# A step order for each engine, high halves first, and hand-overs by blocks of 128 tokens in a four-layer graph network kernel

## The chip, the cores and the metric

The kernel runs on one core of one Trainium2 chip. The metric is the device time of one execution in microseconds, as the median of several runs.

## The reference

`x` has 128 batches of 64 nodes with 256 features. `adj` is one 64 x 64 matrix for all batches. Four layers follow one another, each inside a residual sum and a layer norm:

```python
x = _layernorm(x + _L0_gnn_ref(x, adj, ...))   # aggregate, dense 256->512, batch norm, relu, dense 512->256, batch norm
x = _layernorm(x + _L1_gnn_ref(x, adj, ...))   # L_norm @ x @ Wc, layer norm, relu; 4-head attention; layer norm; gelu MLP; layer norm
x = _layernorm(x + _L2_gnn_ref(x, adj, ...))   # two adj @ (x @ Wg) layers, then LSTMs over windows of 1, 2, 3 and 4 nodes
x = _layernorm(x + _L3_gnn_ref(x, adj, ...))   # graph attention: softmax of masked leaky-relu logits, times Wh
return x
```

The LSTMs run one after another over windows of p = 1 to 4 nodes; the last state of each window replaces the window's last node, so window length p reads what p - 1 wrote.

## The kernel before

**Stages.** Tokens (batch x node) are handled in tiles of 512. Two first stages do layer 0, whose batch norms need sums over all tokens; neither is touched by the change. The third stage, from 242 us to the end, does everything else for 16 tiles: two streams (`s` = 0, 1) of 8 tiles each (`n` = 1 to 8), each tile in two halves (`h` = 0, 1, written `.0` and `.1`) of 256 tokens, each half being two blocks `b` of 128 tokens.

**Products.** Operands of TensorE are pairs of fp16 numbers, a high half and a low half. `product` issues three matmuls for each product: high x high, high x low, low x high. ScalarE writes the high half of an activation from PSUM (`high`, L1447), VectorE then subtracts it and writes the low half (`low`, L1682), and TensorE waits for the low half before its first matmul. The LSTM states are split in the same way by VectorE alone (L1788, L1790 and L1796, the last two after the first).

**Steps and their order.** The work of a half tile is cut into steps: `turn_y` (transposes), `cheb` (the product with `L_norm`), `conv`, `turn_x1`, `v`, `q`, `k`, `scores`, `exps`, `turn_probs`, `attend`, `attn_out`, `turn_x2`, `mlp_up`, `mlp_down`, `mix0`, `gcn0`, `mix1`, `gcn1`, then for 11 LSTM cells c `inpC` (products with the input), `cellC` (products with the state, then gates) and `hidC` (new state), with `packC` for some, then `turn_state`, `turn_xc`, `gat`, `gat_keys`, `gat_exps`, `turn_att`, `gat_mix`, and the layer norms `norm_...`. An entry `1:conv.1` is step `conv` of stream 1, half 1; `+` in place of `:` means the stream's next tile. One list, written out by hand, gives the order for all engines: every engine walks through `OPENING`, seven times through `ROUND` and through `CLOSING`, and does its own part of each step. The engines wait for one another by semaphores (`Signal`); each engine's own instructions run in the order of the list. The two streams are about half a tile apart, so that one has attention while the other has LSTM cells.

**Hand-overs.** A signal covers a half tile where the change touches it: `ln_apply` on VectorE (L1642, two instructions, one for each block) signals after the second, and the TensorE step that reads both blocks waits for it. The same holds for `make_x2` (L1661), for the masked logits (L1811), the exponentials (L1538, ScalarE) and `take_att` (L1544, one copy for both blocks) of graph attention. `gat_mix` (L1393) writes both blocks of a half to one PSUM bank.

Of the kernel before, what the change touches and what calls it, by code (L numbers as in the profile page):

```python
# [82 lines left out]
1:attn_out.0 0:pack4.0 0:hid7.1 1:norm_g2.0 1:mlp_up.1 0:inp8.1 1:gelu_split.1 0:inp7.0 0:cell8.1 1:turn_x2.0
1:mlp_down.1 0:cell7.0 0:hid8.1 0:inp9.1 0:hid7.0 1:norm_g3.1 1:mlp_up.0 1:gelu_split.0 0:cell9.1 1:norm_l1.1 0:inp8.0
0:hid9.1 0:cell8.0 1:mlp_down.0 1:mix0.1 0:inp10.1 0:hid8.0 1:norm_g3.0 0:cell10.1 1:gcn0.1 0:hid10.1 1:norm_l1.0
0:inp9.0 0:cell9.0 1:mix1.1 0:hid9.0 0:turn_state.1 0:inp10.0 1:gcn1.1 0:cell10.0 0:norm_l2.1 0:hid10.0 1:mix0.0
1:inp0.1 0:turn_xc.1 0:turn_state.0 1:cell0.1 1:gcn0.0 0:gat.1 0:norm_l2.0 1:mix1.0 0:gat_keys.1 1:hid0.1 0:turn_xc.0
0:gat_exps.1 1:gcn1.0 1:inp1.1 0:turn_att.1 1:cell1.1 0:gat_mix.1 1:hid1.1 0:gat.0 0:norm_l3.1 1:inp0.0 0+turn_y.1
1:cell0.0 0:gat_keys.0 1:inp2.1 1:cell2.1 0+norm_l0.1 0:gat_exps.0 1:hid0.0 1:hid2.1 1:inp1.0 0:turn_att.0 0+cheb.1
1:cell1.0 0:gat_mix.0 1:inp3.1 1:hid1.0 0:norm_l3.0 0+conv.1 0+turn_y.0 1:cell3.1 1:inp2.0 0+norm_l0.0 0+norm_g1.1  # L90
1:cell2.0 0+cheb.0 1:hid2.0 0+xa_bias.1 1:inp3.0 0+conv.0 0+turn_x1.1 0+norm_g1.0 1:cell3.0 0+v.1 0+xa_bias.0 0+q.1
# [11 lines left out]
0+hid2.1 0+inp3.1 1:norm_l3.1 1+norm_g1.0 0+inp2.0 0+cell2.0 1+turn_y.1 0+cell3.1 1+norm_l0.1 0+hid2.0 0+hid3.1  # L103
0+inp3.0 1+xa_bias.0 1+turn_x1.0
""".split()
ROUND = [(int(entry[0]), int(entry[1] == "+"), entry[2:]) for entry in ROUND]


OPENING = """
# [1824 lines left out]
```

## Time and profile before

| | |
|---|---|
| median of 3 runs | 2045.37 us (2044.44 to 2046.44) |
| the profiled execution, its time | 2043.5 us |
| its span | 2041.7 us |
| TensorE busy in the span | 1947.0 us, 95% |
| VectorE busy | 1721.9 us, 84% |
| ScalarE busy | 1449.9 us, 71% |
| mean granted TensorE clock | 0.994 |

PE is TensorE's matmuls and PEld its weight loads, which run beside them. DVE is VectorE, ACT ScalarE, POOL GpSimd. A matmul's bar is drawn from its start to its modelled end, and bars of successive matmuls overlap.

### The profile page before, as it was taken

What the parts mean: (1) busy time and instruction counts of PE and PEld (TensorE: products, weight loads), DVE (VectorE), ACT (ScalarE), POOL (GpSimd) and SP (SyncE); (2) the same over time, 40 slices, a digit from 0 to 9 for tenths busy, and PEclk for the clock granted to TensorE, in tenths of its full rate; (3) what the DMA queues carried; (4) which work ended last, traced back from release to release, by engine and by line L of the source; (5) the groups of instructions that cost most, each with busy time, mean ns of one, the idle gap of its engine ahead of it and who ended that gap; (6) DMA issues with size and microseconds to landing.
All of it is one profiled execution on the core that took longest, in us unless ns stands there. A gap on an engine that the chain in (4) does not pass through costs nothing.

```text
span 2041.7 us, 85679 instructions
## 1 busy us (share of the span) xinstructions
PE 1947.0 (95%) x37031; PEld 1729.0 (85%) x37031; DVE 1721.9 (84%) x4795; ACT 1449.9 (71%) x4443; POOL 185.9 (9%) x258
## 2 busy tenths in 40 slices
PE   6999879999999999999999999999999999999997
PEld 3444458989998999999998999899989999899996
DVE  6779787889888988898888988898889888888866
ACT  5657536777777787768777777677776777677677
POOL 2000010010101000100011010101010001011000
PEclk9999989999999999999999999999999999999999
DMA  7857400000100001000100010000100010000000
GB/s 283 289 184 267 155 2 23 13 13 3 44 3 23 3 3 44 13 13 3 44 14 13 3 44 3 23 3 3 44 13 13 3 44 13 13 4 13 3 3 23
DMA packets 36822, 87.79 MB, mean 43 GB/s; under 512 B 2416, under 2 KB 26992, under 8 KB 32752
## 3 DMA queue, kind: packets, MB, share of 16 engines
q1 hardware_dynamic: 36464, 82.56, 11.6%
q8 instruction: 280, 4.59, 0.9%
q14 instruction: 78, 0.64, 0.1%
HBM read 52.15 MB, written 30.41 MB: 40 GB/s over the span
## 4 chain that ended last, share of the span: by engine, by line
PE 69%; DVE 11%; ACT 5%; issue 2%; POOL 1%; DVEq 0%; ACTq 0%
PE ps L282 21%; PE ps L284 20%; PE ps L283 20%; ACT pool_mem L1498 2%; DVE stats L1632 2%; PE ps L296 2%; PE ps L1157 2%; PE ps L1240 1%; ACT xb L1434 1%; PE ps L1265 1%; DVE pool_mem L1785 1%; POOL rstd L1596 1%; DVE mv L1636 1%; PE ps L1393 1%; DVE t L1826 1%
## 5 line engine op out<-in xcount | busy, mean ns | idle before, releaser
L1498 ACT ACTIVATE pool_mem<-ps,lstm_b 128x64 f32<-128x64 f32 (+2 forms) x2496 | 610.9, 356 | 96.3 <-PE ps L284 91.9
L282 PE MATMUL ps<-hl_a,w_hi 128*128 128x64 f16 (+2 forms) x3776 | 540.4, 214 | 18.0 <-DVE hl_a L660 16.1
L283 PE MATMUL ps<-hl_a,w_hi 128*128 128x64 f16 (+2 forms) x3776 | 539.5, 214 | 0.0
L284 PE MATMUL ps<-hl_a,w_lo 128*128 128x64 f16 (+2 forms) x3776 | 539.5, 214 | 0.0
L282 PEld LDWEIGHTS ps<-hl_a,w_hi 128*128 128x128 f16 x3776 | 349.2, 97 | 46.1 <-DVE hl_a L660 17.2
L284 PEld LDWEIGHTS ps<-hl_a,w_lo 128*128 128x128 f16 x3776 | 348.8, 97 | 23.0 <-issue 0.7
L283 PEld LDWEIGHTS ps<-hl_a,w_hi 128*128 128x128 f16 x3776 | 348.9, 97 | 22.5 <-issue 0.6
L282 PE MATMUL ps<-hl_b,w_hi 128*128 128x84 f16 (+2 forms) x2112 | 366.0, 228 | 0.3
L283 PE MATMUL ps<-hl_b,w_hi 128*128 128x84 f16 (+2 forms) x2112 | 366.3, 228 | 0.0
L284 PE MATMUL ps<-hl_b,w_lo 128*128 128x84 f16 (+2 forms) x2112 | 365.0, 228 | 0.0
L282 PE MATMUL ps<-pool_mem,w_hi 128*128 128x64 f16 (+2 forms) x3072 | 352.9, 200 | 0.1
L283 PE MATMUL ps<-pool_mem,w_hi 128*128 128x64 f16 (+2 forms) x3072 | 352.6, 200 | 0.0
L284 PE MATMUL ps<-pool_mem,w_lo 128*128 128x64 f16 (+2 forms) x3072 | 352.2, 200 | 0.0
L1596 POOL TENSOR_TENSOR rstd<-mv,nhalf 128x2 f32<-128x2 f32 x224 | 172.1, 770 | 1624.1 <-DVE mv L1636 1624.1
L282 PEld LDWEIGHTS ps<-pool_mem,w_hi 128*128 128x128 f16 x3072 | 284.9, 98 | 2.7 <-DVE pool_mem L1790 0.2
L283 PEld LDWEIGHTS ps<-pool_mem,w_hi 128*128 128x128 f16 x3072 | 286.8, 98 | 0.5
L284 PEld LDWEIGHTS ps<-pool_mem,w_lo 128*128 128x128 f16 x3072 | 285.0, 98 | 0.0
L282 PEld LDWEIGHTS ps<-hl_b,w_hi 128*128 128x128 f16 x2112 | 207.1, 98 | 18.3 <-DVE hl_b L1682 2.0
L284 PEld LDWEIGHTS ps<-hl_b,w_lo 128*128 128x128 f16 x2112 | 206.2, 98 | 14.9
L283 PEld LDWEIGHTS ps<-hl_b,w_hi 128*128 128x128 f16 x2112 | 205.6, 97 | 15.2
L1507 ACT ACTIVATE pool_mem<-pool_mem 128x256 f32<-128x256 f32 (+2 forms) x352 | 128.3, 374 | 82.3 <-DVE pool_mem L1766 44.5
L1632 DVE BATCH_NORM_STATS2 stats<-t 128x6 f32<-128x256 f32 x448 | 168.3, 418 | 5.5
(237 smaller groups left out, 4207.4 us busy)
## 6 DMA issues: line engine op xcount, KB each, us to landing
xa<-in_x SPq DMA_DIRECT2D x32, 512.0 KB, 5.5
h_scratch<-pool_mem SPq DMA_DIRECT2D x14, 1024.0 KB, 4.3
pool_mem<-h_scratch SPq DMA_DIRECT2D x14, 1024.0 KB, 7.0
pool_mem<-in_wpack SPq DMA_DIRECT2D x16, 704.0 KB, 4.2
out<-xb SPq DMA_DIRECT2D x16, 512.0 KB, 3.4
...
```

The source lines that it names most:

```text
L282: nc.tensor.matmul(o, l[0], r[0], start=first, stop=False, skip_group_check=True)
L283: nc.tensor.matmul(o, l[0], r[1], start=False, stop=False, skip_group_check=True)
L284: return nc.tensor.matmul(o, l[1], r[0], start=False, stop=last, skip_group_check=True)
L296: mm = nc.tensor.matmul(to(f, batch)[c, :], of(f)[n, c], matrix[n, n], start=True, stop=True)
L1157: mm = nc.tensor.transpose(fea(s, bank)[:, f, b * P:(b + 1) * P], src[s][:, h * HALF + b, f * P:(f + 1) * P], ident[:, :])
L1240: mm = nc.tensor.matmul(to[half, b, pair, batch * NODES:(batch + 1) * NODES], q[s][h][d, pair, at_b:at_b + NODES], kk[s][h][d, pair, at_b: ...
L1265: mm = nc.tensor.matmul(ps[s][d, banks[batch], c:c + NODES], vv[s][h][k, b, head * HEAD_DIM:(head + 1) * HEAD_DIM], prob_tr[s][h][k, b, pa ...
L1393: mm = nc.tensor.matmul(tok(s, BANK_A[h])[:, b, :], att_tr[s][h][:, b, :], wh[s][h][:, b, :], start=True, stop=True)
L1498: op = nc.scalar.activation(gates[s][h][:, g, m * w:(m + 1) * w], gate_place(s, h, g, m, w), ACT.Tanh, bias=lstm_b[:, bias:bias + 1], scal ...
L1507: nc.scalar.activation(cell_t[s][h][:, 0:KT * w], cell_c[s][h][:, 0:KT * w], ACT.Tanh, scale=0.5)\
L1596: nc.gpsimd.tensor_tensor(rstd[s][:, blocks(h)], mv[s][:, blocks(h), 1], nhalf[:, 0:HALF], ALU.pow)\
L1632: nc.vector.bn_stats(stats[s][:, b, 0:6], t[s][:, b, :]).then_inc(ln_step.of(s, h), 1)
```

## The change

The three lists become one dictionary `ORDER` with a list for each of PE, ACT, DVE and POOL. Each list has three parts: the first for tile 1, the second for each of tiles 2 to 6, and the third for tiles 7 and 8, which are now ordered together. The steps are the same, and so are the matmuls and their number. The middle part keeps every engine's old order apart from local shifts: of PE's 164 entries none moves by more than four places, of the 178 of ScalarE only `norm_y` by more than four (13 later for stream 0, 57 earlier for stream 1), of the 204 of VectorE only `1:cell3.1` by more than five (13 later).

```diff
-ROUND = """
-1:cheb.1 0:pack3.1 0:cell3.0 0+norm_y 1:conv.1 0:inp4.1 0:hid3.0 1:norm_g1.1 0:cell4.1 1:v.0 0:pack3.0 1:q.0 1:k.0
...
+ORDER = {
+    "PE": ("""
+0:turn_y.1 0:turn_y.0 1:turn_y.1 0:cheb.1 1:turn_y.0 0:conv.1 0:cheb.0 0:conv.0 0:turn_x1.1 0:v.1 0:q.1 0:k.1
+0:turn_x1.0 0:scores.1 1:cheb.0 0:v.0 0:q.0 0:k.0 1:cheb.1 0:scores.0 0:turn_probs.1 0:attend.1 0:attn_out.1
+0:turn_probs.0 1:conv.0 0:attend.0 0:turn_x2.1 0:attn_out.0 0:mlp_up.1 1:conv.1 0:turn_x2.0 0:mlp_down.1 0:mlp_up.0
...
+1:cheb.1 0:cell3.0 1:conv.1 1:v.0 1:q.0 1:k.0 0:inp4.1 1:scores.0 1:turn_x1.1 0:inp4.0 1:v.1 1:q.1 1:k.1 0:inp5.0
+1:scores.1 0:inp5.1 0:cell5.1 0:cell5.0 1:turn_probs.1 1:turn_probs.0 0:inp6.1 1:attend.0 1:attend.1 0:cell6.1
...
+1:inp0.0 0:gat_keys.0 0+turn_y.1 1:inp2.1 1:inp1.0 0:turn_att.0 0+cheb.1 0:gat_mix.0 1:inp3.1 0+conv.1 0+turn_y.0
+1:inp2.0 1:cell3.1 0+cheb.0 1:inp3.0 0+turn_x1.1 0+conv.0 1:cell3.0 0+v.1 0+q.1 0+turn_x1.0 0+k.1 0+v.0 0+scores.1
...
+1:turn_xc.0 1:cell10.1 1:gat.0 0+gcn0.0 1:gat_keys.0 1:turn_state.1 0+mix1.0 0+gcn1.1 0+gcn1.0 1:turn_att.0
+1:gat_mix.0 1:turn_xc.1 0+inp0.1 1+turn_y.0 0+inp0.0 1:gat.1 0+inp1.1 1:gat_keys.1 1+cheb.0 0+inp1.0 1+conv.0
...
+    begin, again, end = ORDER[engine]
+    steps = at(begin, 1)
+    for r in range(2, ROUNDS - 1):
+        steps += at(again, r)
+    return steps + at(end, ROUNDS - 1)
...
+                        wait_hi(k)
+                        for b in range(HALF):
                             a = first + b * P
-                            mm = product(tok(s, bank)[:, b, :], (src[:, 0, k, a:a + P], src[:, 1, k, a:a + P]),
-                                         weight(name, k, 0, DIM), k == 0, k == kts - 1 and with_row is None)
...
+                            for part in range(2):
+                                nc.tensor.matmul(tok(s, bank)[:, b, :], hi, w[part], start=k == 0 and b == 0 and part == 0,
+                                                 stop=False, skip_group_check=True)
...
+                    for k in range(kts):
+                        wait_lo(k)
+                        for b in range(HALF):
+                            a = first + b * P
+                            mm = nc.tensor.matmul(tok(s, bank)[:, b, :], src[:, 1, k, a:a + P], weight(name, k, 0, DIM)[0],
+                                                  start=False, stop=k == kts - 1 and b == HALF - 1, skip_group_check=True)
...
+                    def wait_hi(k):
+                        if k == 0:
+                            pe.wait_ge(*(feat_lo if which in MIX_BANK else feat_hi).at(s, n, h, which))
...
-                    pe.wait_ge(*cell_dve.at(s, n, h, f"{c - 1}.lo"))
+                    pe.wait_ge(*cell_dve.at(s, n, h, f"{c - 1}.hi"))
+                    low_ok = cell_dve.at(s, n, h, f"{c - 1}.lo")
...
-                    pe.wait_ge(*gat_ok.at(s, n, h, "exps"))
                     for b in range(HALF):
-                        mm = nc.tensor.transpose(gat_bank(s, h, b)[:, TILE - P:TILE], att[s][h][:, b, :], ident[:, :])
-                    mm.then_inc(gat_ps.of(s, h), 1)
+                        pe.wait_ge(*gat_ok.at(s, n, h, f"exps{b}"))
+                        nc.tensor.transpose(gat_bank(s, h, b)[:, TILE - P:TILE], att[s][h][:, b, :], ident[:, :])\
+                            .then_inc(gat_ps.of(s, h), 1)
...
-                        op = nc.vector.tensor_scalar(dst[s][:, b, :], t[s][:, b, :], mv[s][:, b, 0:1], rstd[s][:, b:b + 1],
-                                                     ALU.subtract, ALU.mult)
-                    op.then_inc(ln_out.of(s, h), 1)
+                        nc.vector.tensor_scalar(dst[s][:, b, :], t[s][:, b, :], mv[s][:, b, 0:1], rstd[s][:, b:b + 1],
+                                                ALU.subtract, ALU.mult).then_inc(ln_out.of(s, h), 1)
```

`rows_of`, `gat_dense`, `cell_input` and `cell_state` are split like `dense`: first all matmuls that read the high half, behind a wait for it, then those that read the low half, behind a wait of their own. For the four operands of `MIX_BANK` (`xp`, `o`, `m0`, `m1`) both waits stay on the low half, because the product writes a PSUM bank that VectorE still reads for it. `turn` and `mix` wait for each block of `l0`, `l1`, `l2` and `x2` separately; `gat_keys`, `turn_att`, `take_att`, the exponentials and `gat_mix` signal by block, and `gat_mix` writes block b to bank `gat_bank(s, h, b)`. `take_att` becomes two copies of 128x128.

## Rows read from the trace of the kernel before

**Rows 1.** The page: span, then each engine's busy time; last the chain that ended last.
```profile
span 2041.7 us, 85679 instructions
...
PE 1947.0 (95%) x37031; PEld 1729.0 (85%) x37031; DVE 1721.9 (84%) x4795; ACT 1449.9 (71%) x4443; POOL 185.9 (9%) x258
...
PE 69%; DVE 11%; ACT 5%; issue 2%; POOL 1%; DVEq 0%; ACTq 0%
```
**Rows 2.** Busy us of each engine by stretch: two rounds, third stage's start and end.
```profile
745.71:965.20 219.49, 215.26 (x4386) 202.38 (x4385) 191.18 (x553) 162.59 (x529) 21.62 (x28) 1.00 0.06 17
...
1184.64:1404.10 219.46, 215.24 (x4386) 202.38 (x4385) 191.14 (x553) 162.63 (x529) 21.62 (x28) 1.00 0.06 17
...
1843.00:2041.70 198.70, 182.29 (x3812) 172.03 (x3810) 152.70 (x468) 145.41 (x502) 15.84 (x21) 0.98 0.03 11
...
240.00:306.81 66.81, 46.58 (x546) 36.15 (x545) 51.80 (x135) 21.95 (x41) 7.92 (x11) 0.87 0.03 9
```
**Rows 3.** PE's waits in the round 745.71 to 965.2: total us, times, longest.
```profile
PE ps L1157 <- DVE x L1642: 0.9, 2, 0.7
PE ps L1240 <- ACT pool_mem L1462: 0.8, 1, 0.8
PE ps L1387 <- ACT pool_mem L1538: 0.7, 1, 0.7
PE ps L296 <- ACT t L1484: 0.6, 1, 0.6
PE ps L296 <- DVE xa L1642: 0.5, 2, 0.3
PE ps L1393 <- ACT pool_mem L1544: 0.5, 1, 0.5
```
**Rows 4.** Timeline around one of these waits: start, us, engine, line.
```profile
895.26 0.27 PE L283 MATMUL ps<-hl_b,w_hi 128*128 128x256 f16 x1
895.37 0.27 PE L284 MATMUL ps<-hl_b,w_lo 128*128 128x256 f16 x1
895.68 0.60 ACT L1462 ACTIVATE pool_mem<-ps 128x512 f32<-128x512 f32 x1 [0.36 <-PE ps L284]
...
896.42 0.69 PE L1240 MATMUL ps<-pool_mem 64*64 64x64 f32 x32 [0.78 <-ACT pool_mem L1462]
```
**Rows 5.** The round's groups by line and shape, busy us, mean ns.
```profile
L282 PEld LDWEIGHTS ps<-hl_a,w_hi 128*128 128x128 f16 x448 | 41.3, 97 | 0.5
...
L1682 DVE TENSOR_TENSOR hl_b<-ps,hl_b 128x512 f16<-128x512 f32 x16 | 11.0, 686 | 1.9 <-ACT hl_b L1447 1.9
...
L1538 ACT ACTIVATE pool_mem<-pool_mem,smin 128x128 f32<-128x128 f32 x9 | 3.6, 416 | 0.9 <-DVE smin L1811 0.8
...
L1642 DVE TENSOR_SCALAR x<-t,mv,rstd 128x256 f32<-128x256 f32 x8 | 2.9, 409 | 1.4 <-POOL rstd L1596 1.4
```
**Rows 6.** PE's waits from 240 to 306.8 us.
```profile
PE ps L282 <- DVE hl_a L1682: 5.5, 3, 2.4
PE ps L1157 <- DVE x L1700: 3.6, 1, 3.6
PE ps L296 <- DVE xa L1642: 3.1, 1, 3.1
PE ps L1157 <- DVE x L1661: 2.2, 2, 1.4
PE ps L282 <- DVE hl_b L1682: 1.8, 1, 1.8
PE ps L282 <- DVE pool_mem L1738: 1.2, 1, 1.2
```
**Rows 7.** PE's waits from 1850 us to the end, the longest.
```profile
PE ps L1148 <- DVE pool_mem L1785: 1.8, 2, 1.0
PE ps L1157 <- DVE x L1661: 1.6, 1, 1.6
PE ps L282 <- DVE hl_b L1682: 1.6, 1, 1.6
```
**Rows 8.** Timeline at the start of `turn_probs` of stream 1.
```profile
800.41 0.69 DVE L1722 TENSOR_TENSOR pool_mem<-pool_mem,ssum 128x512 f32<-128x512 f32 x1
...
801.11 0.86 PEld L1250 LDWEIGHTS ps<-ident,pool_mem 128*128 128x128 f32 x8
```
**Rows 9.** Timeline of the last layer norm and store.
```profile
2034.30 4.04 ACT L1434 ACTIVATE xb<-t,nmr,rstd 128x256 f32<-128x256 f32 x8 [1.73 <-DVE nmr L1668]
...
2036.40 2.35 SPq L1117 DMA_DIRECT2D out<-xb  x2
```

More of the change, by code:

```diff
@@ L1 @@
+import itertools
 from contextlib import ExitStack
@@ L83 @@
[L83 to L91, printed above, removed]
-0+turn_x1.0 1:hid3.0 0+k.1 1:hid3.1 0+scores.1 1:pack3.0 0+v.0 0+exps.1 0+q.0 1:pack3.1 0+k.0 1:inp4.0 1:cell4.0
@@ L103 @@
[L103 to L109, printed above, removed]
-0+norm_y 0+turn_y.1 0+norm_l0.1 0+turn_y.0 0+cheb.1 0+norm_l0.0 0+conv.1 1+norm_y 0+norm_g1.1 0+cheb.0 0+xa_bias.1
-0+turn_x1.1 0+conv.0 0+v.1 0+q.1 0+norm_g1.0 0+k.1 0+xa_bias.0 0+scores.1 0+turn_x1.0 1+turn_y.0 0+exps.1 0+v.0
-1+norm_l0.0 0+q.0 0+k.0 0+turn_probs.1 0+scores.0 0+attend.1 0+exps.0 0+attn_out.1 0+norm_g2.1 0+turn_probs.0
@@ new lines @@
+0:inp9.0 0:cell9.0 1:mix1.1 0:inp10.0 0:turn_state.1 0:cell10.0 1:gcn1.1 1:mix0.0 0:turn_xc.1 1:inp0.1 0:gat.1
+0:turn_state.0 0:gat_keys.1 1:gcn0.0 1:inp1.1 1:mix1.0 0:turn_att.1 0:turn_xc.0 0:gat_mix.1 1:gcn1.0 0:gat.0
+1:inp0.0 0+turn_y.1 0:gat_keys.0 1:inp2.1 1:inp1.0 0+cheb.1 0:turn_att.0 1:inp3.1 0:gat_mix.0 0+conv.1 1:inp2.0
+0+turn_y.0 1:cell3.1 0+turn_x1.1 1:inp3.0 0+cheb.0 0+v.1 0+conv.0 0+q.1 1:cell3.0 0+k.1 0+turn_x1.0 0+scores.1 0+v.0
+0+q.0 0+k.0 1:inp4.0 0+scores.0 0+turn_probs.1 1:inp5.0 0+attend.1 1:cell5.0 0+attn_out.1 0+turn_probs.0 1:inp4.1
@@ new lines @@
+1:cell8.1 1:hid8.1 1:turn_state.0 1:norm_l2.0 1:cell9.1 1:hid9.1 1:turn_xc.0 0+mix1.0 1:cell10.1 1:hid10.1
+1:gat_keys.0 0+mix1.1 1:turn_state.1 1:norm_l2.1 1:gat_exps.0 0+gcn1.1 1:gat_mix.0 1:turn_xc.1 1:norm_l3.0 0+cell0.1
+0+gcn1.0 1+turn_y.0 0+hid0.1 1+norm_l0.0 1:gat_keys.1 0+cell1.1 1+cheb.0 0+cell0.0 1:gat_exps.1 0+hid1.1 0+hid0.0
+1+conv.0 0+cell1.0 1:gat_mix.1 0+cell2.1 0+hid1.0 1:norm_l3.1 0+hid2.1 1+norm_g1.0 0+cell2.0 1+turn_y.1 0+hid2.0
+1+norm_l0.1 0+cell3.1 1+xa_bias.0 0+hid3.1 1+turn_x1.0
@@ new lines @@
+1:turn_state.0 1:cell9.1 1:norm_l2.0 1:hid9.1 1:turn_xc.0 0+mix0.0 1:cell10.1 1:hid10.1 0+mix1.1 1:gat_keys.0
+0+mix1.0 1:turn_state.1 1:gat_exps.0 1:norm_l2.1 0+gcn1.1 1:gat_mix.0 0+gcn1.0 1:norm_l3.0 1:turn_xc.1 0+cell0.1
+1+turn_y.0 0+cell0.0 0+hid0.1 1+norm_l0.0 0+hid0.0 0+cell1.1 1+cheb.0 1:gat_keys.1 0+hid1.1 1+conv.0 0+cell1.0
+1:gat_exps.1 0+cell2.1 1:gat_mix.1 0+hid1.0 0+hid2.1 1:norm_l3.1 1+norm_g1.0 0+cell2.0 1+xa_bias.0 1+turn_y.1
+0+cell3.1 1+norm_l0.1 0+hid2.0 0+hid3.1 1+turn_x1.0
@@ L1183, in dense @@
[L1183 to L1193 removed]
+                            hi, w = src[:, 0, k, a:a + P], weight(name, k, 0, DIM)
@@ L1413, in _ @@
                 keep_clock(ps[1][:, 2, :], 6)
[L1414 to L1419 removed]
+                for name, s, n in steps_of("PE"):
                     run(name, s, n)
```

533 lines of the change are left out of this document (358 added, 175 removed).

## The prediction

> **What bounds the kernel now.** I read the page first. Of the span of 2041.7 us TensorE's matmuls fill 95%, VectorE 84% and ScalarE 71%, and the chain that ended last lies on TensorE for 69% [rows 1]. TensorE is the bound, and a change that leaves its matmuls as they are can only take time out of its pauses. The change touches the third stage alone, so I then cut that stage by stretches [rows 2]. A round of the steady part takes 219.5 us, twice alike, with matmuls busy for 215.3: 4.2 us idle. The start, 240 to 306.8 us, has 46.6 us busy out of 66.8, at a mean granted clock of 0.87: 20.2 us idle, and about 0.13 x 66.8 = 8.7 us of clock withheld, which costs only where PE works. The end, from 1843 us, has 182.3 of 198.7: 16.4 us idle. Between 306.8 us and about 2000 us lie some 7.7 rounds.
>
> Third, the view of waits says which pause ends on what. In a steady round it has six groups, eight waits, 4.0 us together [rows 3]. None of them is a wait for a low half: ScalarE's or VectorE's last instruction of another kind ends each. At the start the low halves do appear: 5.5 us of `hl_a`, 1.8 of `hl_b` and 1.2 of `pool_mem` at L1738, out of 17.4 shown [rows 6]. At the end there is 1.6 [rows 7].
>
> The waits are too small by one piece each. In the timeline the last matmul before `scores` starts at 895.37 us. Its like follow one another after 0.11 us, yet its bar is 0.27 long, and `scores` starts at 896.42 [rows 4]. So 1.05 - 0.11 = 0.94 us were lost where the view counts 0.78: 0.16 us more for each wait. Eight waits then cost 4.0 + 8 x 0.16 = 5.3 us a round.
>
> **The change, part by part.** It removes no matmul and adds none; both parts of a product keep their weight loads.
>
> (a) The step order and the block hand-overs in a steady round. I go through [rows 3] with the new lists beside them.
> The 0.8 of `scores` behind `take_k` (L1462): the new PE list has `0+v.0` between `0+k.1` and `0+scores.1`, twelve matmuls of 0.11 us, 1.3 us of work. The wait goes.
> The 0.9 behind L1642 is `turn_xc` after `norm_l2`: `1:gat_mix.0` now comes before `1:turn_xc.1`, and the first block is signalled one instruction of 0.41 us earlier [rows 5]. About 0.3 is left.
> The 0.7 behind L1538 is `turn_att` after the exponentials: its first block is signalled one activation of 0.42 us earlier [rows 5], and the masked logits before it by one instruction. About 0.1 is left.
> The 0.6 behind L1484 is `mix1` after `gcn_relu`: `1:turn_state.1`, four transposes of 0.11 us each [rows 8], moves in front of `0+mix1.0`. About 0.15 is left.
> The 0.5 behind `xa` is `cheb` after `norm_l0`, two waits of 0.3 or less, and a block is 0.41 us earlier. About 0.1 is left.
> The 0.5 behind L1544 is `gat_mix` after `take_att` of half 1: `1:gcn1.0` now stands between. But `1:turn_att.0` and `1:gat_mix.0` now stand side by side where `turn_xc.1` had been between, and the copy, though halved, has to be waited for. About 0.45 stays.
> Kept 1.1 of 4.0; saved 2.9, and for four or so waits that vanish 4 x 0.16 = 0.6: 3.5 us a round. Over 7.7 rounds 27 us. The bounds are nothing (each wait comes back elsewhere) and all 5.3 us, 41 us.
>
> (b) High halves first. A low half of 512 elements takes VectorE 0.69 us [rows 5], and TensorE may now start that much sooner after the high half. In the steady round no wait ends on a low half [rows 3], because other steps of the hand-made order stand in between and hide the 0.69 us. So I book nothing there; what hides it is TensorE's own work, and if the tighter rounds of (a) use up that cover, the earlier start is what keeps the wait from appearing. Where TensorE does wait for one, at the start for `hl_b` and `pool_mem`, I book two times 0.7 = 1.4 us [rows 6]. The largest, 5.5 us for `hl_a`, is `xp` and `o`, which belong to `MIX_BANK` and still wait for their low half: nothing.
>
> (c) The start. The new PE list moves one `turn_y`, `cheb.0`, `cheb.1`, `conv.0` and `conv.1` of stream 1 into places where stream 0's chain had left TensorE idle. A `conv` is twelve matmuls of 0.11 us, 1.3 us, a transpose or mixing step some 0.7: together 4.7 us of work that no longer has to be done later. Signals by block take 0.4 us from each of three waits, for `xa` and L1661 [rows 6]: 1.2. With (b) that is 7.3 us. Against it, VectorE is already busy for 51.8 of 66.8 us there [rows 2], and the layer norm that goes before a moved `cheb` costs it some 3 us, in front of stream 0's own chain in the same queue. I take 2 us off: 5 us saved. ScalarE's `norm_y` of the next tile of stream 0 now stands early, behind `cheb.1`. It needs the first load, for which the queue waits only until both `turn_y` are done, and it is two ScalarE instructions in a stretch where that engine is busy 22 of 67 us [rows 2]: nothing. The bounds for the start are minus 3 us (VectorE's work wholly in the chain) and 20 us (all idle time).
>
> (d) The end. Tiles 7 and 8 in one list let stream 0's last cells fill stream 1's gaps. The last layer norms and the store, 2034.3 us to the end, 7.4 us, stay [rows 9], so of 16.4 us idle 9 can be had; waits of 1.8, 1.6 and 1.6 lead them [rows 7]. I take 3 us, with bounds of 0 and 9.
>
> (e) Added work. `take_att` becomes two copies, one more ScalarE instruction for each half tile, 32 in all. ScalarE is idle for 57 us of a round [rows 2]: nothing.
>
> The Trainium skill has a rule that speaks against the signals by block: "TensorE: Matmul & The Clock Gate", section "The cost: per-tile semaphore tail", gives 26.3 ns for each increment that a matmul makes and advises one on the last. The change has 12 more a round, by that figure an estimated 0.3 us a round and 2.5 us over the kernel; no run here shows it yet, and the sum leaves it out.
>
> **Sum.** 27 + 5 + 3 = 35 us. The profiled execution took 2043.5 us, so 2008.5. Its time lies 1.9 us below the median of the runs, so for the median 2010 us. The bounds of the terms add up to minus 3 and 41 + 20 + 9 = 70 us, 1975 to 2048.
>
> **Rivals.** One: half of the gain comes back. When TensorE's round shrinks to 216 us, VectorE is busy for 191 of it [rows 2], 89%, and both it and ScalarE have in-order queues. Each handover that they make late shows up as a new short wait. For it: four of the six groups of waits already end on ScalarE or on VectorE work behind it, not on any missing TensorE work. Against it: VectorE and ScalarE get lists of their own, so a ready instruction is less often held behind another. The price is half of the 27 us or more: 2024 to 2041 us.
>
> Two: there is more to gain than the waits show. Weight loads are busy 202.4 us of a round, so 17.1 us have none [rows 2], four times the idle time of the matmuls. Some of that is not a pause: a load takes 0.097 us [rows 5] under a matmul of 256 columns that takes 0.11. If half of the 13 us that the two figures differ by is real pause, and high-first and the new lists take half of that, 3 us a round more go, 25 us in all: about 1985 us, and below.
> The Trainium skill, "Perfetto Trace Analysis", section "Identifying the Most-Contended Engine", says that matmul busy share is a poor measure of how near TensorE is to its limit and that weight loads are the better one; it is the page for this rival. By matmuls a round could give 4.2 us, by loads up to 17.1.
>
> Three: it gets slower. The lists of different engines contradict each other in places. In the middle part PE does `1:turn_probs.1` before `1:turn_probs.0`, while VectorE and ScalarE make `exps.0` and `turn_probs.0` first. Before, the last multiplication ended at 801.10 us and the eight transposes began at 801.11 without a wait, half 0 first [rows 8]: what is now asked for first had 0.4 us to spare, four transposes. With nothing ready behind it, TensorE waits for all of the difference. A place of this kind costs 0.7 us, a VectorE instruction [rows 5]. It takes more than five of them a round before the 3.5 us saved are lost, and with eight a round is 2.1 us longer, 16 us in all: 2053 us once the 8 us of start and end are taken off. It decides from the sixth on.
>
> Four: no change, 2041.3 to 2049.5 us. A measurement tells 0.2%, 4.1 us, from nothing. All the terms would have to be at their low ends.
>
> **Chances.** My forecast, 1990 to 2024 us: 0.60. Rival one, 2024 to 2041: 0.17. Rival two, below 1990: 0.10. No change: 0.05. Slower: 0.08. Faster by over 0.2% is 0.60 + 0.17 + 0.10 = 0.87. Leaving out some 0.07 at the low side, the part of rival two below 1983, and some 0.13 above, the two last cases, the range is 1983 to 2040 us.
>
> **What the profile after would show.** A round of 215 to 217 us between repeats of one instruction; PE's waits in it without L1240 and L1484, those for L1642 and L1538 below 0.4, and one for the copy of `take_att` of stream 1 half 0. In the start, from 242 us to the first LSTM gates, a stretch 4 to 7 us shorter with less time at the half clock. The number of matmuls the same, 37031. The prediction is wrong if the round is not shorter (rivals one and three: look for new waits, `turn_probs` first), or shorter by more than 6 us (rival two: pauses that the matmul bars had hidden).

## The result, and the profile after

The changed kernel takes 2014.85 us, the median of 4 runs (2013.94 to 2015.3), against 2044.9 us of the kernel before (4 runs, 2044.25 to 2046.44): a ratio of 0.9852, with a 95% interval of 0.9838 to 0.9866. It is 30.0 us faster. The forecast was 2010 us, a gain of 35. The profiled execution took 2013.94 us, at a mean granted clock of 0.996 (0.994 before).

The page of the changed kernel: span, busy times, and the chain that ended last by engine.

```profile
span 2012.1 us, 85711 instructions
...
PE 1944.8 (97%) x37031; PEld 1730.6 (86%) x37031; DVE 1718.2 (85%) x4795; ACT 1443.6 (72%) x4475; POOL 187.8 (9%) x258
...
PE 78%; ACT 5%; DVE 4%; issue 1%; POOL 0%; ACTq 0%; DVEq 0%
```

Beside [rows 1] the matmuls are the same 37031, and the busy times of TensorE, VectorE and ScalarE stay within 0.5% (GpSimd's within 1%); ScalarE has the 32 instructions more that the halved copies make. VectorE's share of the last chain falls from 11% to 4%, TensorE's rises from 69% to 78%. Of the 29.6 us by which the span shrank, TensorE's idle time gives 27.4 and its busy time 2.2: its work stayed the same, its pauses shrank.

Windows of the changed kernel: a steady round from one instruction to its repeat, then the same 66.8 us at the start as in [rows 2], and last a stretch of about the same length at the end. The columns are those of [rows 2]. The next round, to 1276.60 us, takes 215.72 us.

```profile
845.17:1060.88 215.71, 214.54 (x4386) 202.70 (x4384) 190.91 (x553) 161.93 (x533) 21.84 (x28) 1.00 0.06 18
...
240.00:306.81 66.81, 51.82 (x681) 40.19 (x680) 58.60 (x153) 26.78 (x50) 10.37 (x13) 0.92 0.08 25
...
1813.00:2012.10 199.10, 182.44 (x3798) 172.31 (x3796) 150.41 (x466) 144.53 (x507) 15.35 (x21) 0.98 0.03 11
```

This round takes 215.7 us where it took 219.5, and TensorE's idle time in it falls from 4.2 to 1.2 us. The start now holds 681 matmuls in the 66.8 us that held 546, at a mean granted clock of 0.92 instead of 0.87. The last 199 us look as before: 16.7 us idle, 16.4 before.

TensorE's waits in this round, all of them:

```profile
PE ps L1330 <- DVE x L1859: 0.6, 1, 0.6
PE ps L1627 <- ACT pool_mem L1772: 0.2, 1, 0.2
```

These two lines answer to the six of [rows 3]. L1330 is `turn_xc` behind `norm_l2`. L1627 is `gat_mix` behind the copy of `take_att`, at 949 us, where `1:turn_att.0` and `1:gat_mix.0` stand side by side. The waits of `scores`, `mix1`, `cheb` and `turn_att` are gone. No wait stands at `turn_probs`, the place that rival three named.

The timeline around the longer one shows who is late.

```profile
1058.10 0.69 DVE L1898 TENSOR_TENSOR hl_b<-ps,hl_b 128x512 f16<-128x512 f32 x1
...
1058.70 0.72 DVE L1859 TENSOR_SCALAR x<-t,mv,rstd 128x256 f32<-128x256 f32 x2
...
1059.16 0.33 PE L1330 MATMUL ps<-ident,x 128*128 128x128 f32 x1 [0.65 <-DVE x L1859]
```

TensorE needs the first block of a layer norm (L1859), and VectorE makes the low half of another stream's product (L1898, 0.69 us) ahead of it. Block hand-over shows too: TensorE starts at 1059.16, before the second of the two instructions ends at 1059.42.

TensorE's waits from 240 to 306.8 us, the longest and those of the kinds that stood in [rows 6]:

```profile
PE ps L1353 <- DVE hl_a L1898: 5.3, 5, 1.8
PE ps L468 <- DVE xa L1859: 2.5, 1, 2.5
...
PE ps L1330 <- DVE x L1916: 0.8, 1, 0.8
...
PE ps L1353 <- ACT pool_mem L1707: 0.8, 2, 0.4
...
PE ps L1330 <- DVE x L1877: 0.4, 1, 0.4
PE ps L1363 <- DVE hl_b L1898: 0.4, 1, 0.4
```

The 5.3 us for `hl_a` are the low halves of `xp` and `o` and, at 298.66 us, of `m0`, which still are waited for. (The prediction put the 5.5 us of [rows 6] down to `xp` and `o` alone; the third of them, at 305.38 us, is `m0`, which belongs to `MIX_BANK` as well.) The 1.2 for the gelu's low half became 0.8 for its high half (ScalarE's L1707), and the 1.8 for `hl_b` 0.4. The 3.6 and 2.2 us behind VectorE's L1700 and L1661 became 0.8 and 0.4 (L1916 and L1877).

TensorE's waits from 1850 us to the end, the longest, and then the last layer norm and the store in the timeline:

```profile
PE ps L1320 <- DVE pool_mem L2002: 2.6, 2, 2.3
PE ps L1330 <- DVE x L1877: 2.0, 1, 2.0
PE ps L1627 <- ACT pool_mem L1772: 1.2, 2, 1.0
```
```profile
2003.15 4.04 ACT L1662 ACTIVATE xb<-t,nmr,rstd 128x256 f32<-128x256 f32 x8 [0.98 <-DVE nmr L1884]
...
2007.21 0.93 SPq L1289 DMA_DIRECT2D out<-xb  x2
```

The three longest are no shorter than those of [rows 7]; all of the view together are 6.0 us against 7.4. The last layer norm's eight instructions take 4.04 us on ScalarE as in [rows 9], but what follows does not stay. In [rows 9] the first store is issued 2.10 us after the first of the eight starts, here 4.06 us after it. ScalarE's old list ends `0+norm_l3.1 0+norm_l3.0 1+norm_l3.1 1+norm_l3.0`, so stream 0's tile is complete after four of the eight; the new one ends `0+norm_l3.1 1+norm_l3.1 1+norm_l3.0 0+norm_l3.0`, and a store needs both halves of its tile. From the first of the eight to the end are 9.0 us where there were 7.4.

**Where the 30 us lie.** From the two traces, from instruction to its repeat, and last from that layer norm to the end of the span:

| stretch | before | after | difference |
|---|---|---|---|
| third stage's start to the first `gcn` relu | 65.1 | 59.7 | -5.4 |
| from there to the first `norm_l3` | 120.1 | 117.1 | -3.0 |
| five repeating rounds | 5 x 219.48 | 5 x 215.96 | -17.6 |
| the round after them | 219.4 | 217.1 | -2.3 |
| from there to the last layer norm | 290.2 | 288.7 | -1.5 |
| from the last layer norm to the end | 7.4 | 9.0 | +1.6 |
| the third stage | 1799.7 | 1771.4 | -28.3 |

The third stage starts at 242.0 us before and at 240.7 after. Both executions run the same code up to there, and in other executions it starts at up to 244.7, so these 1.3 us, which with the 28.3 make the 29.6 of the spans, are no part of the change. The start's own length also varies: from the stage's first instruction to the first `gcn` relu, two kernels below with the same first lists take 62.1 and 64.2 us (e1 and e6), and four with the new ones 57.6 to 59.7 (e5, e8, e9 and the changed kernel).

### The profile page after: what moved, and what is told of

Its sections match the earlier page's. It is cut to its first block, busy times and chain, and to the rows that moved or that the text cites. A ratio compares the mean times of both kernels' runs of the same rounds, so it can differ in the third digit from the quotient of the medians.

```text
span 2012.1 us, 85711 instructions
## 1 busy us (share of the span) xinstructions
PE 1944.8 (97%) x37031; PEld 1730.6 (86%) x37031; DVE 1718.2 (85%) x4795; ACT 1443.6 (72%) x4475; POOL 187.8 (9%) x258
## 4 chain that ended last, share of the span: by engine, by line
PE 78%; ACT 5%; DVE 4%; issue 1%; POOL 0%; ACTq 0%; DVEq 0%
PE ps L1539 18%; PE ps L1568 11%; PE ps L1548 9%; PE ps L1353 8%; PE ps L1387 7%; PE ps L1575 5%; PE ps L1363 4%; PE ps L1395 3%; PE ps L468 2%; PE ps L1330 2%; ACT pool_mem L1726 2%; PE ps L1320 1%; PE ps L1627 1%; PE ps L1595 1%; PE ps L1441 1%; DVE stats L1849 1%
## 5 line engine op out<-in xcount | busy, mean ns | idle before, releaser
L1539 PE MATMUL ps<-hl_a,w_hi 128*128 128x64 f16 (+1 forms) x3584 | 361.3, 205 | 1.8 <-DVE hl_a L2005 0.9
L1539 PE MATMUL ps<-hl_a,w_lo 128*128 128x64 f16 (+1 forms) x3584 | 360.8, 205 | 0.0
L1539 PEld LDWEIGHTS ps<-hl_a,w_hi 128*128 128x128 f16 x3584 | 284.4, 97 | 6.3 <-DVE hl_a L2005 1.2
L1568 PE MATMUL ps<-pool_mem,w_hi 128*128 128x64 f16 (+2 forms) x3072 | 273.6, 200 | 0.0
L1548 PE MATMUL ps<-hl_a,w_hi 128*128 128x64 f16 (+1 forms) x3584 | 233.5, 205 | 0.2 <-issue 0.2
L1568 PEld LDWEIGHTS ps<-pool_mem,w_hi 128*128 128x128 f16 x3072 | 228.9, 98 | 2.9
L1548 PEld LDWEIGHTS ps<-hl_a,w_hi 128*128 128x128 f16 x3584 | 177.4, 97 | 0.9 <-issue 0.3
L1575 PE MATMUL ps<-pool_mem,w_hi 128*128 128x64 f16 (+2 forms) x3072 | 175.4, 200 | 0.0
L1983 DVE SCALAR_TENSOR_TENSOR pool_mem<-pool_mem 128x256 f32<-128x256 f32 (+2 forms) x352 | 118.8, 340 | 38.7 <-ACT pool_mem L1726 36.4
L1387 PE MATMUL ps<-hl_b,w_hi 128*128 128x256 f16 x640 | 150.3, 273 | 0.4 <-DVE hl_b L1898 0.2
L1387 PE MATMUL ps<-hl_b,w_lo 128*128 128x256 f16 x640 | 150.2, 273 | 0.0
L2002 DVE SCALAR_TENSOR_TENSOR pool_mem<-pool_mem 128x256 f32<-128x256 f32 (+2 forms) x352 | 123.9, 356 | 28.9 <-ACT pool_mem L1735 27.8
L1575 PEld LDWEIGHTS ps<-pool_mem,w_hi 128*128 128x128 f16 x3072 | 135.9, 98 | 0.0
L1539 PE MATMUL ps<-hl_b,w_hi 128*128 128x84 f16 x1408 | 130.4, 201 | 0.5
L1539 PE MATMUL ps<-hl_b,w_lo 128*128 128x84 f16 x1408 | 130.5, 200 | 0.0
```

The costliest lines, as they stand in the source:

```text
L1387: nc.tensor.matmul(out[:, j, :], w[part], hi[:, k, :], start=j == 0 and k == 0 and part == 0, stop=False, skip_group_check=True)
L1539: nc.tensor.matmul(o, wk[part], toks[0][:, k], start=(g, m) == gms[0] and k == 0 and part == 0, stop=False, skip_group_check=True)
L1548: mm = nc.tensor.matmul(o, weight(f"wih{p}", k, (g * KT + m) * P, P)[0], toks[1][:, k], start=False, stop=step == 0 and (g, m) == gms[-1] ...
L1568: nc.tensor.matmul(gate_place(s, h, g, m, w), wk[part], hi[:, k * w:(k + 1) * w], start=False, stop=False, skip_group_check=True)
L1575: mm = nc.tensor.matmul(gate_place(s, h, g, m, w), weight(f"whh{p}", k, (g * KT + m) * P, P)[0], lo[:, k * w:(k + 1) * w], start=False, st ...
L1983: nc.vector.scalar_tensor_tensor(cc if first else g[GATE_I], g[GATE_I], 1.0, g[GATE_G], ALU.add, ALU.mult).then_inc(cell_dve.of(s, h), 1)
```

## The experiments

Each experiment takes the changed kernel and edits it, and none leaves out any of the computation. "Round" is the mean of the five repeating rounds in the trace.

### The first four: which part of the change carries the gain

`e1_old_order` puts back the old lists and keeps high-first and the blocks:

```diff
-ORDER = {... "PE": ("""0:turn_y.1 0:turn_y.0 1:turn_y.1 0:cheb.1 1:turn_y.0 ...
+ORDER = {... "PE": ("""0:turn_y.1 0:turn_y.0 0:cheb.1 0:conv.1 0:cheb.0 ...   (all four lists cut from the old ROUND)
```

> The changed kernel with the one hand-written step order of before put back on all engines; high halves first and hand-overs by block stay. Theory (the step orders carry most of a round's gain, block hand-overs some, high halves first next to nothing in a round): only what the block signals shorten is kept, about 0.4 us for each of the waits behind L1642, L1538 and xa, 1.2 to 1.6 us a round, 9 to 12 us, and 2 to 3 us at the start: 2031 to 2035 us, a round of 218 us. Rival (high halves first carries it): most of the 30 us stay, 2015 to 2023 us. Rival (nothing without the new orders): 2042 to 2045 us.

`e2_low_first` keeps the lists and the blocks, and lets each high matmul wait for the low half, as before:

```diff
-    pe.wait_ge(*(feat_lo if which in MIX_BANK else feat_hi).at(s, n, h, which))
+    pe.wait_ge(*feat_lo.at(s, n, h, which))
...
-    pe.wait_ge(*cell_dve.at(s, n, h, f"{c - 1}.hi"))
+    pe.wait_ge(*cell_dve.at(s, n, h, f"{c - 1}.lo"))
...
-    pe.wait_ge(*gelu_hi.at(s, n, h, f"m{k + KT - 1}"))
+    pe.wait_ge(*gelu_lo.at(s, n, h, "m23" if k else "m01"))
```

> The changed kernel, but TensorE waits for the low half before the first matmul of each product, as before the change; the new order of the matmuls inside a product, the new step orders and the hand-overs by block stay. Theory: the low halves were hidden in a round, so a round stays within 0.3 us of 215.7 and only the start loses 1.4 us: 2016 to 2019 us. Rival (the new step orders are tighter and need the earlier start): each product of a short cycle waits up to 0.7 us, 1 us or more a round, 2023 us or more.

`e3_half_signals` keeps the lists and high-first; each wait for a block becomes a wait for the second block:

```diff
-    turn(s, n, h, xc, "xc", lambda b: pe.wait_ge(*ln_out.at(s, n, h, f"l2.{b}")))
+    turn(s, n, h, xc, "xc", lambda b: pe.wait_ge(*ln_out.at(s, n, h, "l2.1")))
...
-    pe.wait_ge(*gat_ok.at(s, n, h, f"exps{b}"))
+    pe.wait_ge(*gat_ok.at(s, n, h, "exps1"))
```

> The changed kernel, but every wait for a block waits for the second block of the half tile (layer norms l0, l1, l2, x2, keys, masked logits, exponentials, take_att, gat_mix); the instructions and their signals stay as they are. Theory: the waits that remain in a round grow by up to 0.4 us each, 0.8 to 1.2 us a round, and the start by 1 us: 2021 to 2025 us. Rival (blocks are worth nothing, since other work hides the 0.4 us): 2014 to 2016 us.

`e4_order_alone` is the new lists with the edits of both e2 and e3.

> The new step orders alone: both undoings of the two runs before together. Theory: 2022 to 2028 us, the two losses add up, and with the run on the old order the three parts sum to the whole 30 us within 5 us. Rival (the parts need one another): above 2035 us, or the sum of the parts misses the whole by 10 us or more.

Measured, all four on one chip, against 2045.97 us of the kernel before there:

| kernel | median us | ratio (95%) | round us |
|---|---|---|---|
| e1_old_order | 2037.22 | 0.9964 (0.995 to 0.9978) | 218.85 |
| e2_low_first | 2070.44 | 1.0119 (1.0103 to 1.0134) | 222.4 |
| e3_half_signals | 2028.58 | 0.9914 (0.9901 to 0.9928) | 217.11 |
| e4_order_alone | 2080.95 | 1.0171 (1.0157 to 1.0185) | 223.4 |

All four missed the ranges expected of them: e1 by 2 us and e3 by 4, e2 and e4 by over 50. e2 and e4 refuted the theory behind the prediction. Without high-first the new lists are not a little less good, they lose 25 us to the kernel before, and without the blocks 35 us. TensorE's waits in a round of e2 say why:

```profile
PE ps L1353 <- DVE pool_mem L1940: 1.8, 3, 0.8
PE ps L1531 <- DVE hl_a L1883: 1.7, 3, 0.8
PE ps L1330 <- DVE x L1844: 0.6, 1, 0.6
PE ps L1557 <- DVE pool_mem L1992: 0.6, 2, 0.4
PE ps L1531 <- DVE hl_a L1998: 0.4, 1, 0.4
PE ps L1353 <- DVE hl_b L1883: 0.3, 1, 0.3
PE ps L1612 <- ACT pool_mem L1757: 0.2, 1, 0.2
```

Five of these seven lines, ten waits and 4.8 us, or 6.4 us with 0.16 more for each, end on a low half made by VectorE: of the gelu (L1940), of `h1`, the input of the LSTM windows of one node (`hl_a`, L1883; TensorE's L1531 is in `cell_input`), of `x1` in front of `v` (`hl_b`, L1883), of the LSTM state (L1992, L1998). In [rows 3] there is none of this kind. The round is 6.4 us longer than the changed kernel's 215.96. The new lists put products closer behind what feeds them: between `1:gcn1.1`, from which `h1` comes, and `1:inp0.1` the old list has `0:cell10.0` and `1:mix0.0`, the new one `0:cell10.0` alone. The other two lines are the waits that the changed kernel has too, at the same length. The longest of the three for `h1` in the timeline:

```profile
874.02 0.23 PE L1531 MATMUL ps<-hl_a,w_hi 128*128 128x128 f16 x1 [0.82 <-DVE hl_a L1883]
```

In e1 the waits of the old order are back:

```profile
PE ps L1235 <- ACT pool_mem L1484: 0.8, 1, 0.8
PE ps L262 <- ACT t L1506: 0.6, 1, 0.6
PE ps L1415 <- ACT pool_mem L1560: 0.5, 1, 0.5
PE ps L1124 <- DVE x L1653: 0.4, 1, 0.4
PE ps L1181 <- DVE hl_b L1692: 0.3, 1, 0.3
PE ps L1421 <- ACT pool_mem L1566: 0.2, 1, 0.2
```

`scores` keeps its 0.8 and `mix1` its 0.6, since no block signal touches them. `turn_xc` (L1124) goes from 0.9 to 0.4, `turn_att` (L1415) from 0.7 to 0.5, and `gat_mix` (L1421) from 0.5 to 0.2. So the blocks give part of these and the order the rest. The 0.3 at L1181 is new: it is `gcn1`, whose operand `m1` belongs to `MIX_BANK` and is waited for in its low half.

In e3 the layer norm's wait is 1.0 instead of 0.6, the copy's 0.5 instead of 0.2, and `turn_att` behind the exponentials (L1621) and `cheb` (L468) have waits again:

```profile
PE ps L1330 <- DVE x L1859: 1.0, 1, 1.0
PE ps L1627 <- ACT pool_mem L1772: 0.5, 1, 0.5
...
PE ps L1621 <- ACT pool_mem L1766: 0.2, 1, 0.2
PE ps L468 <- DVE xa L1859: 0.2, 1, 0.2
```

By the medians the blocks are worth 13.7 us here (2028.58 to 2014.85), which is more than expected. In the third stages of the two traces it is 11.9 us: 1.15 us in each of five rounds, 4.3 us in the last two tiles (293.0 us against 288.7), 1.1 behind the last layer norm and 0.7 in the round before. The rest is a third stage that starts 2.0 us later in e3's execution.

### The other corners: is anything gained or lost under the old order

`e10_old_high_first` is e1 with the half-tile waits of e3. `e11_old_all_undone` adds the low-half waits of e2. What is then left of the change is the order of the matmuls within a product, the additional signals and the split copy.

> High halves first alone: the old step order, and every wait for a block waits for the second block. The run with new orders and low halves waited for first was 55 us slower than the changed kernel, so high halves first is worth much under the new orders. Theory now (the old order had hidden the low halves behind other steps, the new orders spend that cover): here it is worth 0 to 0.3 us a round and the few us of the start, 2040 to 2045 us. Rival (it is worth a like amount under either order, and something else in the run with low halves first cost the time): 2000 us or less.

> A control: the changed kernel with all three parts undone, the old step order, low halves waited for first, waits for whole half tiles. What is left of the change is the order of the matmuls inside a product (all high ones, then all low ones), take_att in two copies, the bank of gat_mix and one signal for each block. Theory: these cost and give nothing that a run can tell, 2044 to 2048 us. Rival (the order of the matmuls itself, or the additional signals, cost time: then the runs with low halves first are slow for this reason): 2055 us or more.

Measured beside 2046.13 us: e10 2046.02 us, ratio 1.0 (0.9991 to 1.0009), round 219.65; e11 2045.61 us, ratio 1.0002 (0.9993 to 1.0011), round 219.55. e11 is as expected; e10, at 2040 to 2045 us expected, is 1 us above its range, and gained nothing at all. Under the old order high-first is worth nothing that the medians show, and the other orders within a product, the signals and the copy cost nothing. With the changed kernel itself the runs so far make a table of medians:

| | low half first, half signals | low first, blocks | high first, half signals | high first, blocks |
|---|---|---|---|---|
| old lists | 2045.6 (e11) | not run | 2046.0 (e10) | 2037.2 (e1) |
| new lists | 2081.0 (e4) | 2070.4 (e2) | 2028.6 (e3) | 2014.9 (after) |

The rows compare runs on several chips, on which the kernel before took 2044.9 to 2046.13 us, and the third stage starts up to 4 us apart in them; a difference between two cells is good to a few us.

From low to high first: 0 under the old lists, 52 and 56 us under the new ones. Blocks: 9 under the old lists, 10.5 and 13.7 under the new. The lists themselves: 35 us worse with low first and half signals, 17 us better with high first, 22 better with high first and blocks. The third stages of the traces give the same picture without the stretch ahead of them: high first 2.5 us under the old lists and 52 and 54 under the new; blocks 10, then 10 and 12; the lists 33 us worse, 17 better and 19 better. The parts do not add up; the lists and high-first are one change.

### Which low half matters

`e12_low_first_cells` lets products of the LSTM cells wait for the low half: the packs, the inputs of windows of 2 and the states. The inputs of windows of one node, which read `h1`, stay high first. `e13_low_first_gelu` lets only `mlp_down` wait. Both have the new lists and the blocks.

```diff
 # e12
-    pe.wait_ge(*cell_act.at(s, n, h, f"pack{p}.{step}"))
+    pe.wait_ge(*cell_dve.at(s, n, h, f"pack{p}.{step}"))
...
-    pe.wait_ge(*cell_dve.at(s, n, h, f"{c - 1}.hi"))
+    pe.wait_ge(*cell_dve.at(s, n, h, f"{c - 1}.lo"))
 # e13
-    pe.wait_ge(*gelu_hi.at(s, n, h, f"m{k + KT - 1}"))
+    pe.wait_ge(*gelu_lo.at(s, n, h, "m23" if k else "m01"))
```

> The changed kernel, but the products of the LSTM cells alone wait for the low half before their first matmul (packs, inputs of windows of 2, states). The run with low halves first everywhere was 55 us slower, its round 6.4 us longer, and its timeline shows the lost time at cell inputs (0.98, 0.67, 0.52, 0.49 us), at states (0.56, 0.43), at mlp_down (0.94, 0.71, 0.61) and at conv or attn_out products (0.46). Theory: each place costs what it shows, the cells about half, 2.5 to 3.5 us a round, 20 to 30 us: 2035 to 2045 us. Rival (the cells' splits are 0.3 us long and others hide them): under 2022 us.

> The changed kernel, but mlp_down alone waits for the low half of the gelu output before its first matmul. Theory: three waits, 2.2 us a round, 15 to 18 us: 2029 to 2033 us. Rival (removing one wait only lets the next be longer, so that one undone part costs little): under 2020 us.

Measured beside 2045.52 us: e12 2026.26 us (0.9908, 0.9894 to 0.9923), round 217.42; e13 2041.19 us (0.9978, 0.997 to 0.9987), round 218.82. Both expectations missed, in opposite directions: what e12 edits of the cells is worth 11 us, `mlp_down` 26. The waits of e12's round (without the 0.2 of the `take_att` copy, which is as before), and then of e13's:

```profile
PE ps L1330 <- DVE x L1859: 0.6, 1, 0.6
PE ps L1568 <- DVE pool_mem L2007: 0.6, 2, 0.4
PE ps L1539 <- DVE hl_a L2013: 0.4, 1, 0.4
```
```profile
PE ps L1353 <- DVE pool_mem L1955: 2.5, 3, 1.0
PE ps L1330 <- DVE x L1859: 0.6, 1, 0.6
PE ps L1627 <- ACT pool_mem L1772: 0.2, 1, 0.2
```

e12 missed because its expectation counted places that its edit does not touch. Of the four cell inputs in it, 0.98, 0.67 and 0.49 us are e2's three waits for `h1` (0.82, 0.51 and 0.32 in the timeline, and 0.16 more). The input and the two states that are left make 0.52 + 0.56 + 0.43 = 1.5 us, and e12's round is 1.46 us longer than the changed kernel's. So the rule that each place costs what it shows held.

The timeline of e13 at the longest of the three new waits (start, us, engine, line):

```profile
919.89 0.52 ACT L1707 ACTIVATE pool_mem<-ps,col 128x256 f16<-128x256 f32 x1
...
920.23 0.88 DVE L1877 SCALAR_TENSOR_TENSOR x<-t,rstd,row 128x256 f32<-128x256 f32 x2
...
921.02 1.30 DVE L1955 TENSOR_TENSOR pool_mem<-pool_mem 128x512 f16<-128x512 f32 x2
921.77 0.28 PE L1353 MATMUL ps<-w_hi,pool_mem 128*128 128x256 f16 x1 [1.05 <-DVE pool_mem L1955]
```

ScalarE has the high half at 920.41. VectorE makes the low half only at 921.02 to 921.67, because its queue still holds a layer norm of 0.88 us. So the high-first start is worth, at this place, not the 0.65 us of one VectorE instruction, but that instruction and whatever stands ahead of it in VectorE's queue: the high half comes from ScalarE, and waits for nothing of VectorE. The three waits, 2.5 us and 0.16 us more for each, make 3.0 a round; the round is 2.86 longer. The start is 6.6 us longer as well (183.4 against 176.8 us to the first `norm_l3`).

The two together cost 11.4 + 26.3 = 37.7 of the 55.6 us that e2 loses. Of a round's 6.4 us, 1.5 and 2.9 are theirs and 2.1 are left. What neither run touched are the low halves that L1883 makes: the three waits for `h1` at the cells' inputs, 1.7 us in e2's view and 2.1 with 0.16 more for each, and one of 0.3 for `x1` in front of `v`. So most of the other 18 us belongs to the LSTM cells too, which makes the cells as a whole worth at least as much as `mlp_down`. This is by subtraction and e2's waits only; no run has `h1` alone, and the parts need not add up: `mlp_down`'s three waits are 1.8 us in e2's view and 2.5 in e13's.

### Where the lists pay

`e6_new_middle` has the new lists only in the five repeating rounds, `e5_new_start` only in the first part; the other parts are the old lists. High-first and blocks are kept.

```diff
-"PE": (new_begin, new_again, new_end)
+"PE": (old_begin, new_again, old_end)      # e6, the same for ACT, DVE and POOL
+"PE": (new_begin, old_again, old_end)      # e5
```

> High halves first and block hand-overs, with the new lists for the five middle rounds only; the first and last parts of every list are the old order. Beside the run on the old order throughout, 2037.2 us with a round of 218.85. Theory: five rounds of 215.9 us instead, 2.9 each, 14.5 us: 2022 to 2024 us, with a round of 215.7 to 216. Rival (the new round only holds when the streams enter it at the distance that the new start sets): a round above 217 us and 2030 us or more.

> High halves first and block hand-overs, with the new lists for the first part only, which holds the start and the first round; all later rounds and the end in the old order. Theory: the start is 5 us shorter than with the old order, as the two traces show up to the first layer norm of layer 3, and the first round gains some 2 more: 2030 to 2033 us beside 2037.2. Rival (the next round in the old order gives it back, since VectorE's work was only moved ahead): 2036 us or more.

e6: 2024.62 us (0.9896, 0.9881 to 0.9911), round 216.21. e5: 2029.58 us (0.9922, 0.9908 to 0.9935), round 218.60. e6 is 0.6 us above its range and e5 0.4 below, and neither rival came true. Against e1 (2037.22) the middle lists give 12.6 us and the start lists 7.6; of the 22.4 that all lists give, 2.2 would be left for the end.

The traces say that the end gets nothing of it. From the first `norm_l3` of the seventh round to the end of the span the kernel before takes 297.6 us. e1 and e6, which have high-first and blocks with the old last lists, take 295.4, and the changed kernel, with the new ones, 297.6 again. So at the end high-first and blocks gain 2.2 us and the new last lists lose them: 0.6 us up to the last layer norm and 1.6 behind it, where both stores now come late. The difference in the medians is in good part that e1's third stage starts 3.9 us later than the changed kernel's; from its start to the end the lists give 18.9 us, not 22.4. The old last lists with the rest of the changed kernel, which should take 2.2 us less by these traces, weren't run.

### What one wait costs, and what follows when one is taken away

`e9_scores_back` exchanges one pair in TensorE's list, in the first part and in the repeating one, so that `scores` stands right behind `k` again.

```diff
-0+k.1 0+v.0 0+scores.1
+0+k.1 0+scores.1 0+v.0
```

> The changed kernel with one pair swapped back in TensorE's list, in the first part and the five middle rounds: 0+scores.1 before 0+v.0, as before the change. It prices one wait by itself. Theory (a wait is lost in full, by what the timeline shows and not only by what the view of waits counts): 0.94 us each, six times, 5.6 us: 2020 to 2021 us, the wait for ScalarE's take_k back with 0.8 us in the view. Rival (the chain has slack elsewhere and swallows it): under 2017 us.

`e8_norm_l2_sooner` exchanges one pair in VectorE's list: the layer norm that TensorE still waits for comes before the low half of 1:mix1.0, as it did in the old list.

```diff
-1:mix1.0 0:norm_l2.0
+0:norm_l2.0 1:mix1.0
```

> The changed kernel with one pair swapped in VectorE's middle list, five rounds of the seven: the apply of 0:norm_l2.0 before the low half of 1:mix1.0. It aims at the longest wait left in a round, 0.6 us before 0:turn_xc.0. Theory (PE is the bound, so what a wait loses comes off the round): 0.4 to 0.7 us a round, 2 to 3.5 us in all, 2011 to 2013 us beside 2014.9. Rival (the swapped low half of m1 is now late by its 0.7 us in place): no change or up to 3 us slower.

Both were measured beside 2046.13 us. e9: 2022.03 us (0.9889, 0.9874 to 0.9903). The median lies 1 us above the expected range, in runs from 2018 to 2026 us. A round is 216.90 us, 0.94 longer than the 215.96 of the changed kernel (0.84 to 1.07 in the five rounds one by one), and the waits of its round are those two of the changed kernel and one more:

```profile
PE ps L1235 <- ACT pool_mem L1484: 0.8, 1, 0.8
PE ps L1124 <- DVE x L1653: 0.6, 1, 0.6
PE ps L1421 <- ACT pool_mem L1566: 0.2, 1, 0.2
```

The view says 0.8 and the round lost 0.94, which is what [rows 4] had given by hand for this wait: 0.78 + 0.16. The third stage is 7.0 us longer, where six such waits make 5.6; 1.4 us lie outside what this wait explains.

e8: 2016.64 us (0.986, 0.9845 to 0.9875), no different from the changed kernel; 2011 to 2013 us had been expected. Its five rounds take 215.80 us on the mean against 215.96. The waits of a round:

```profile
PE ps L1421 <- ACT pool_mem L1566: 0.2, 1, 0.2
PE ps L1124 <- DVE x L1653: 0.2, 1, 0.2
```

The layer norm's wait shrank from 0.6 to 0.2, as intended, but only 0.16 us of the 0.4 reached the round. The timeline shows what came next:

```profile
1062.11 0.76 PE L1124 MATMUL ps<-ident,x 128*128 128x128 f32 x4 [0.18 <-DVE x L1653]
...
1062.33 0.40 ACT L1560 ACTIVATE pool_mem<-pool_mem,smin 128x128 f32<-128x128 f32 x1
...
1062.73 0.39 ACT L1560 ACTIVATE pool_mem<-pool_mem,smin 128x128 f32<-128x128 f32 x1
1062.88 0.14 PEld L1415 LDWEIGHTS ps<-ident,pool_mem 128*128 128x128 f32 x1 [0.25 <-ACT pool_mem L1560]
...
1063.27 0.14 PEld L1415 LDWEIGHTS ps<-ident,pool_mem 128*128 128x128 f32 x1 [0.25 <-ACT pool_mem L1560]
```

TensorE is done with the transposes of `turn_xc` and comes to `turn_att` while the exponentials are still running: its weight loads wait 0.25 us for the first and 0.25 for the second. In the changed kernel's round the exponentials hold up one load only, by 0.2. The view of the matmuls' waits shows nothing of this, since under the bars of the matmuls before it there is no gap; the loads' view does. The expectation counted the wait as if nothing were late behind it. The rival's time came true, but not its mechanism: no wait for the low half of `m1` is in view, and the median's 1.8 us more than the changed kernel's lie ahead of the third stage, which starts at 244.2 us in e8's execution against 240.7 and takes 1770.9 us against 1771.4.

## Why the prediction was right, and where its reasons were not

The time was right within 5 us (2014.85 against 2010), and so were the sign and the range. By the third stage alone, without the 1.3 us of its earlier start, the gain is 28 us against the 35 forecast. Step by step:

**The bound.** Right. TensorE's busy time changed by 0.1%, and the pauses gave 27.4 of the 29.6 us.

**(a), per round.** Right in size: 3.5 us forecast, 3.5 measured (219.48 to 215.96). What is left was 1.1 us by forecast and is 0.8: `scores`, `cheb`, `mix1` and `turn_att` have none, the copy of `take_att` waits where it was said to, 0.2 instead of 0.45, and `turn_xc` keeps 0.6 instead of 0.3. The 0.3 was reckoned from TensorE's list alone; in VectorE's new list a low half stands ahead of that layer norm, which it follows in the old one. The additional 0.16 us of each wait was confirmed by e9.

**(a), number of rounds.** The term of the sum that was too large: 3.5 x 7.7 = 27 us. Only five rounds gave 3.5; with the stretch before them, 3.0, and the one behind, 2.3, it is 22.9 us in 6.5 rounds. The other 1.2 of the 7.7 rounds lie in the last stretch, which gave nothing in all. The stretches that use the first and the last list have other waits than a steady round, and they had been multiplied by its price.

**(b), high halves first: the step whose reason failed.** "So I book nothing there", because no wait of [rows 3] ends on a low half. That was right of the kernel before: e10 shows 0 us. It was wrong of the changed one, where high-first is worth 52 to 56 us (e3 against e4, after against e2). The sum came out right because (a) was read from a list of waits without low halves, and so held the value of (b) in it without saying so: the 3.5 us a round are there only while high-first keeps the ten waits of e2 away. The half sentence on the cover being used up named this, but as a footnote to a term of nothing, not as the condition for the other term. With the new lists alone the kernel is 35 us slower than before; the expectation for e4, made from the prediction's terms, was some 20 us faster.

**(c), the start.** 5 us forecast, 5.4 measured, with the clock in the first 66.8 us at 0.92 instead of 0.87. The match is closer than this stretch can be measured, since it varies by 2 us between executions with the same first lists. e5 puts the lists' share of the whole first part at 7.6 us.

**(d), the end.** 3 forecast, none measured: 1.5 us up to the last layer norm, and 1.6 lost behind it. Its longest waits moved and did not shrink: 1.8, 1.6 and 1.6 in [rows 7], 2.6, 2.0 and 1.2 now. "The last layer norms and the store ... 7.4 us, stay" was wrong: they take 9.0, because the new last lists finish both tiles together. And the 1.5 us come from high-first and blocks, not from tiles 7 and 8 in one list, as e1 and e6 show.

**(e) and the signals.** Nothing, as booked: e11 has the split copy, the extra signals and the other matmul order, and a ratio of 1.0002. The Trainium skill, "TensorE: Matmul & The Clock Gate", section "The cost: per-tile semaphore tail", gives 26.3 ns for an increment, by which the estimate was 2.5 us. e11's ratio of 1.0002 reaches to 1.0011 at most, 2.3 us, so the 2.5 us are not borne out for this pattern, in which these increments are us apart, unless something else that e11 keeps saves as much.

**Rival one** (half of the gain comes back) names what e8 and the wait of `turn_xc` show, short waits behind VectorE, but they took back nothing like half. **Rival two** (more than the waits show) is not borne out: the round is 215.7, not 213 or less. Weight loads fill 202.5 of it, 94%, and 13 us a round still have none, while the waits in view have come down to 0.8. The rule on weight loads in the Trainium skill ("Perfetto Trace Analysis", section "Identifying the Most-Contended Engine") didn't tell the room for this change: here the waits in view, with 0.16 us added to each, did. **Rival three** (lists that contradict each other) has no wait at `turn_probs`. A slower outcome was close by, though, through a mechanism that no rival named: products standing too close behind the low halves that they read.

**What stays open.** Which engine's list carries the gain: no run mixes one engine's old list with the others' new ones. The 18 us that e12 and e13 leave, `h1` and `x1`, were found by subtraction alone. Low first with blocks under the old lists wasn't run, nor were the old last lists with the new first and middle ones.
